# New call orders on four engines in a pre-norm attention and mixture-of-experts kernel, and a bias written four times by its transfer

## The reference

```
def _L0_attn_ref(x, Wq, Wk, Wv):
    q = jnp.einsum('bnd,de->bne', x, Wq)
    k = jnp.einsum('bnd,de->bne', x, Wk)
    v = jnp.einsum('bnd,de->bne', x, Wv)
    scores = jnp.einsum('bqe,bke->bqk', q, k)
    scores = jnp.where(causal, scores, -jnp.inf)
    attn = jax.nn.softmax(scores / jnp.sqrt(jnp.float32(k.shape[-1])), axis=-1)
    return jnp.einsum('bqk,bke->bqe', attn, v)

def _L0_ffn_ref(x, shared_gate, shared_up, shared_down, gate_w, up_w, down_w, router_w, routing_bias):
    shared = down(silu(gate(x)) * up(x))              # one expert for all tokens
    logits = jnp.einsum('bsh,eh->bse', x, router_w) + routing_bias
    scores, indices = jax.lax.top_k(jax.nn.sigmoid(logits), 2)
    scores = scores / jnp.sum(scores, axis=-1, keepdims=True)
    ...                                               # the two chosen of 8 experts, weighted
    return shared + combined

x = x + _L0_attn_ref(_layernorm(x), Wq, Wk, Wv)
x = x + _L0_ffn_ref(_layernorm(x), ...)
```

## Time and profile before

| | us |
|---|---|
| median of three runs | 547.94 |
| lowest and highest of them | 544.14, 548.08 |
| the profiled execution | 547.93 |
| its span | 546.2 |
| TensorE busy in the span | 512.3 (94%) |
| VectorE, ScalarE, GpSimd busy | 323.0, 308.4, 283.1 |

### The profile page before, as it was taken

How to read it: one execution, slowest core, us unless ns; L and a number is a source line. 1 busy time by engine, 2 the same in 40 slices (tenths; PEclk the granted TensorE clock), 3 DMA queues, 4 the chain that set the end, 5 groups by cost and what they waited for, 6 DMA issues and landing times.

```text
span 546.2 us, 15135 instructions
## 1 busy us (share of the span) xinstructions
PE 512.3 (94%) x4869; PEld 423.5 (78%) x4869; DVE 323.0 (59%) x918; ACT 308.4 (56%) x588; POOL 283.1 (52%) x237
## 2 busy tenths in 40 slices
PE   4798998899999999999999999999999999999992
PEld 3465776688887888888767789888798888888881
DVE  4788999688988788898645334334243332343331
ACT  3889896678877757675243444444444433444341
POOL 3347776768787765865033244353533525345444
PEclk9899999899999999999999999999999999999997
DMA  8399875989694967446558675665854756446443
GB/s 266 77 223 181 171 180 107 197 251 198 179 199 141 199 171 123 133 149 188 134 91 106 83 110 74 90 82 77 105 69 72 82 64 89 57 66 79 61 61 38
DMA packets 139351, 68.55 MB, mean 126 GB/s; under 512 B 114608, under 2 KB 132336, under 8 KB 139280
## 3 DMA queue, kind: packets, MB, share of 16 engines
q1 hardware_dynamic: 126128, 48.84, 45.7%
q0 software_dynamic: 13152, 18.76, 19.6%
HBM read 19.46 MB, written 23.08 MB: 78 GB/s over the span
## 4 chain that ended last, share of the span: by engine, by line
PE 68%; DMA 8%; DVE 7%; ACT 5%; SPq 5%; issue 4%; POOL 2%; POOLq 0%; ACTq 0%; DVEq 0%
PE bank L2252 31%; PE bank L2276 16%; PE bank L2585 4%; PE bank L2358 3%; PE bank L2383 2%; PE bank L2602 2%; PE bank L2405 2%; PE bank L2663 2%; DMA x<-rows 2%; PE bank L2428 2%; SPq L420 2%; DMA v<-xnrow 2%; DMA wst<-w_all 1%; DMA ptr<-phl 1%; DMA xn2t<-xrow 1%
## 5 line engine op out<-in xcount | busy, mean ns | idle before, releaser
L2252 PE MATMUL bank<-xn2t,w 128*128 128x256 f16 x1608 | 185.5, 273 | 1.6 <-DVE th L1676 1.3
L2252 PEld LDWEIGHTS bank<-xn2t,w 128*128 (+1 forms) x1608 | 155.3, 98 | 22.7 <-DVE th L1676 1.9
L1676 DVE SCALAR_TENSOR_TENSOR th<-th,bank 128x512 f32<-128x512 f32 x83 | 56.8, 685 | 68.7 <-ACT th L1002 64.5
L2276 PE MATMUL bank<-w,h 128*128 (+1 forms) x768 | 92.2, 272 | 0.3
L1002 ACT ACTIVATE th<-bank 128x512 f32<-128x512 f32 x83 | 49.4, 596 | 61.9 <-PE bank L2252 54.6
L2276 PEld LDWEIGHTS bank<-w,h 128*128 128x128 f16 x768 | 73.1, 98 | 9.6 <-issue 0.3
L875 POOL DMA_INDIRECT out<-p,wm x28 | 44.4, 1587 | 65.1 <-ACT p L1333 24.0
L1489 DVE TENSOR_TENSOR h<-th,h 128x512 f16<-128x512 f32 (+1 forms) x69 | 47.1, 683 | 45.2 <-ACT h L952 44.9
L952 ACT ACTIVATE h<-th 128x512 f16<-128x512 f32 (+1 forms) x69 | 42.9, 622 | 53.2 <-DVE th L1676 31.5
L771 POOL DMA_INDIRECT rows<-xrow,sidx x56 | 59.0, 1054 | 16.5 <-issue 13.3
L749 POOL TENSOR_TENSOR w<-wst,w 128x768 f16<-128x768 f32 x32 | 52.7, 1647 | 19.7 <-ACT w L952 19.5
(11 more groups left out here) (193 smaller groups left out, 792.4 us busy)
## 6 DMA issues: line engine op xcount, KB each, us to landing
wst<-w_all SPq DMA_DIRECT2D x36, 384.0 KB, 4.1
x<-x SPq DMA_DIRECT2D x8, 512.0 KB, 5.8
out<-x SPq DMA_DIRECT2D x8, 512.0 KB, 3.8
rows<-x POOLq DMA_DIRECT2D x1, 1192.5 KB, 8.6
rows<-xrow,sidx POOLq DMA_INDIRECT x56
out<-p,wm POOLq DMA_INDIRECT x28
xn2t<-rows SPq DMA_TRANSPOSE x26, 3.9
wm<-rows SPq DMA_DIRECT2D x26, 9.0 KB, 2.6
```

Source lines behind the costliest of these rows:

```text
L1676: d.scalar_tensor_tensor(out=tb, in0=tb, scalar=1.0 / WS if by_silu(t) else 0.5 / (WS * WS), in1=U[half][:, :], op0=ALU.mult, op1=ALU.mult ...
L2252: ins = mm(dst, w_ap(j, ws, m * MAT + k * I + (2 * half + i) * P, P), moving(ms * KD + k), start=(cnt == 0), stop=(cnt == 3 * KD - 1))
L2276: ins = mm(o[:, a * D:(a + 1) * D], hb[:, (hs * KI + i) * TT + a * P:(hs * KI + i) * TT + (a + 1) * P], w_ap(j, ws, 2 * MAT + i * D, D), s ...
```

## The change

TensorE's list is not touched. The bias transfer writes all four copies, has a semaphore of its own (`bias_in`), and is issued after four loads of x; `bias_rows` is gone, and `router_high` waits for the router alone. Everything else is order. In the lists of VectorE, ScalarE, GpSimd and SyncE calls are moved in the opening and in `iteration(i)`; no call but `bias_rows` is added or removed, save one more wait on GpSimd (`shift2`) in the opening. The lists of the last batch and of the routed experts stay.

```
-            sp.dma_start(biases[:, 0:E], bias.partition_broadcast(P)).then_inc(small_in, 16)
             x_load(1)
             w_load(0)
             x_load(2)
+            w_load(1)
             x_load(3)
-            w_load(1)
+            sp.dma_start(biases[:, :].rearrange("p (n e) -> p n e", n=NB),
+                         bias.partition_broadcast(P).unsqueeze(1).to_broadcast([P, NB, E])).then_inc(bias_in, 16)
+            x_load(4)
             xn_transpose(1)
...
             p_transpose(0, 2)
+            xn_transpose(2)
             p_transpose(0, 3)
-            xn_transpose(2)
             w_load(4)
-            x_load(4)
             w_load(5)
...
             p_transpose(1, 2)
+            p_transpose(1, 3)
             w_load(6)
-            p_transpose(1, 3)
-            x_load(5)
-            w_load(7)
             xn2_transpose(0, 0)
             xn2_transpose(0, 1)
+            w_load(7)
+            xn_transpose(3)
             w_load(8)
-            xn_transpose(3)
             p_transpose(2, 0)
+            x_load(5)
             w_load(9)
-            xn2_transpose(1, 0)
             p_transpose(2, 1)
             w_load(10)
+            xn2_transpose(1, 0)
             xn2_transpose(1, 1)
             p_transpose(2, 2)
+            w_load(11)
             p_transpose(2, 3)
-            w_load(11)
             w_load(12)
 
             def iteration(i):
 
+                w_load(4 * i + 1)
                 out_base(i - 3)
-                w_load(4 * i + 1)
                 xn2_transpose(i - 1, 0)
+                xn2_transpose(i - 1, 1)
                 w_load(4 * i + 2)
-                xn2_transpose(i - 1, 1)
                 p_transpose(i, 0)
+                p_transpose(i, 1)
                 xn_transpose(i + 1)
-                p_transpose(i, 1)
                 p_transpose(i, 2)
                 p_transpose(i, 3)
                 w_load(4 * i + 3)
+                x_load(i + 3)
                 w_load(4 * i + 4)
-                x_load(i + 3)
...
@@ GpSimd
             w_low(2)
             w_low(3)
+            rstd1(3)
             rstd2(0)
+            pool.wait_ge(shift2, 1)
             w_low(4)
-            w_low(5)
             xn2_low(0, 0)
             xn2_low(0, 1)
+            w_low(5)
+            rstd1(4)
+            xn_low(3)
             w_low(6)
-            xn_low(3)
             rstd2(1)
-            rstd1(4)
             w_low(7)
...
@@ ScalarE
             exp_of(0, 2)
+            xn_high(2)
             p_high(0, 2)
+            w_scale(2)
+            t_high(1, 0)
             exp_of(0, 3)
-            xn_high(2)
+            t_high(1, 1)
             p_high(0, 3)
-            t_high(1, 0)
-            w_scale(2)
-            t_high(1, 1)
+            w_scale(3)
             w_high(2)
-            w_scale(3)
+            exp_of(1, 0)
             w_high(3)
-            exp_of(1, 0)
+            exp_of(1, 1)
             p_high(1, 0)
-            exp_of(1, 1)
             p_high(1, 1)
             exp_of(1, 2)
+            v_high(1, 0)
+            w_scale(4)
             p_high(1, 2)
-            v_high(1, 0)
             v_high(1, 1)
-            w_scale(4)
             w_high(4)
             t_high(2, 0)
-            w_scale(5)
             exp_of(1, 3)
             p_high(1, 3)
-            w_high(5)
...
-            def bias_rows():
-
-                dve.wait_ge(small_in, 32)
-                for i in range(1, NB):
-                    ins = d.tensor_copy(biases[:, i * E:(i + 1) * E], biases[:, 0:E])
-                ins.then_inc(bias_rdy, 1)
...
@@ VectorE
             first_xn_normalise()
+            stats_1(1)
             wm_low()
-            stats_1(1)
             aggregate_1(1)
...
             t_low(1, 1)
+            p_low(0, 3)
+            row_max(1, 0)
             add_attention(0, 0, 1)
-            row_max(1, 0)
-            bias_rows()
             minus_max(1, 0)
...
             v_low(1, 0)
             shift_2(0)
+            row_sums(1)
             p_low(1, 3)
+            t_low(2, 0)
             v_low(1, 1)
             stats_1(4)
-            t_low(2, 0)
-            row_sums(1)
...
             ffn_gate(1, 1)
             read_logits(1)
+            add_attention(2, 0, 1)
+            p_low(2, 3)
             ffn_up(1, 1)
             add_attention(2, 1, 2)
             route(1)
+            weights(1)
             ffn_low(1, 0)
-            weights(1)
             add_attention(2, 2, 3)
+            add_attention(2, 3, 4)
             add_shared(0)
-            add_attention(2, 3, 4)
-            ffn_low(1, 1)
             stats_2(2)
             aggregate_2(2)
-            places(1)
-            t_low(3, 1)
+            ffn_low(1, 1)
             v_low(3, 0)
             shift_2(2)
+            t_low(3, 1)
+            places(1)
```

More of the change, by code:

```diff
@@ L1168, in _ @@
             xn2_high(0, 1)
-            w_scale(6)
-            w_high(6)
+            w_scale(5)
+            w_high(5)
             xn_normalise(3)
             xn_high(3)
+            w_scale(6)
+            exp_of(2, 0)
+            p_high(2, 0)
             v_high(2, 0)
-            exp_of(2, 0)
+            w_high(6)
+            exp_of(2, 1)
             v_high(2, 1)
-            p_high(2, 0)
-            exp_of(2, 1)
             w_scale(7)
@@ L1206, in _ @@
             xn_normalise(4)
-            xn_high(4)
             w_scale(11)
             w_high(11)
+            w_scale(12)
             v_high(3, 0)
+            xn_high(4)
+            w_high(12)
+            v_high(3, 1)
             t_high(3, 1)
-            v_high(3, 1)
-            w_scale(12)
-            w_high(12)
             xn2_normalise(2, 0)
@@ L1221, in iteration @@
                 exp_of(i, 0)
+                xn2_high(i - 1, 1)
                 p_high(i, 0)
-                xn2_high(i - 1, 1)
                 tanh(2 * i - 4, 0)
+                w_scale(4 * i + 1)
                 exp_of(i, 1)
+                w_high(4 * i + 1)
                 p_high(i, 1)
                 exp_of(i, 2)
-                p_high(i, 2)
                 split_h(2 * i - 4, 0)
@@ L1905, in _ @@
             row_max(0, 1)
+            v_low(0, 0)
             minus_max(0, 1)
+            row_max(0, 2)
             p_low(0, 0)
-            row_max(0, 2)
+            v_low(0, 1)
+            p_low(0, 1)
             minus_max(0, 2)
-            p_low(0, 1)
             row_max(0, 3)
@@ L1913, in _ @@
             p_low(0, 2)
-            v_low(0, 1)
+            row_sums(0)
             aggregate_1(3)
-            row_sums(0)
-            p_low(0, 3)
             t_low(1, 0)
             t_low(1, 1)
+            p_low(0, 3)
+            row_max(1, 0)
             add_attention(0, 0, 1)
-            row_max(1, 0)
-            bias_rows()
             minus_max(1, 0)
```

217 lines of the change are left out of this document (106 added, 111 removed).

## The result

The kernel before has a median of 547.1 us over 19 runs (544.14 to 552.31), the changed one 550.15 over 19 (547.01 to 553.58). The ratio is 1.0063, with a 95% interval from 1.0043 to 1.0082: 3 us slower, where 4.4 faster was forecast. The profiled execution took 552.7 us; its span is 551.0, against 546.2. It is one of the longer ones, 2.6 us above its median, where the profiled one of before is 0.8 above its own: the two profiles differ by 4.8 us and the medians by 3.0, so a part of what the profile shows may be missing in other runs.

A forecast was written before the change was run, and what follows sets the result against it. TensorE bounds the kernel, busy 512.3 of 546.2 us. Terms: 0 at 45, +1.0 at 50, -2.0 at 71, +2.5 at 84, +2.2 and +1.2 at `logits(2)`: 4.9, less 0.5; 547.9 - 4.4 = 543.5 us, range 541 to 545.5.

The forecast's parts named there:

- Iterations 3 to 6 ... Zero.: Iterations 3 to 6: no TensorE idle to gain, about 2.4 us of slack before `pv(4,2)` for later `p_low(i,3)`; zero change.
- its own signs: Wrong if `pv(1,0)` moves over 1.5 us, `logits(2)` still waits 2 us, or TensorE idles in iterations 3 to 6.
- The slower rival: Iterations: work behind `read_logits(i-1)` outlasts the slack, `pv(i,2)` waits 2 us in each of four; 551.5 us, chance 0.13.
- Step 1: Start of the opening: `t_product(0)` some 0.3 us earlier (0 to 0.6); the larger bias transfer costs nothing.
- Step 2: Opening, bias copies removed: up to 1.8 us freed, 0 if GpSimd's hold passes on to `minus_max`.
- Steps 3 and 4: Opening: net 0 (-1.5 to +1.5) at `pv(1,0)` near 45.2; then +1.0 us (0 to 1.4) at `pv(1,3)`, transpose earlier.
- Step 5: Batch 1's `xn2`: transposes behind `w_load(10)` stall `logits(1)`, 1.0 us later than before, a step of -2.0 (0 to -4).
- Step 6: Batch 2's norm: `scores(3)` 1.5 us earlier; at `logits(2)` +2.2 from its wait and +1.2 from the clock drop.

The follow-up runs named there:

- stand-ins: Kernels, before and after included, whose DMA transposes are replaced by plain copies of the same bytes, same queue and semaphores: 540.69 us for before, 546.20 for after.
- h5: Small kernel without the layer, VectorE's subtraction started inside GpSimd's instruction by small operations ahead: six take 1.97 us beside GpSimd's subtraction, fourteen 1.12 beside one indirect DMA.
- s3: Changed kernel's opening with the old iteration order of all four engines, transposes as plain copies: 538.93 us, ratio 0.9848 to the kernel before.
- t2: Changed opening with the old iterations of all four engines again, transposes as plain copies, on another chip: 542.50 us, ratio 0.9803 to the kernel before.
- u2: Changed kernel with GpSimd's `rstd2(i)` moved ahead of `w_low(4i+3)`, transposes as plain copies: 547.01 us, ratio 0.9988 to the kernel before.
- s5: Changed kernel with VectorE's `ffn_low(2i-3,1)` moved back ahead of `weights(i-1)`, transposes as plain copies: 547.28 us, ratio 1.0008 to the kernel before.
- s8: Changed kernel with ScalarE's old iteration order alone, transposes as plain copies: 542.84 us, ratio 0.9899 to the kernel before.
- t3: Changed kernel with ScalarE's `w_scale(4i+1)` and `w_high(4i+1)` moved back to later places, transposes as plain copies: 552.45 us, ratio 1.0010 to the kernel before.
- s7: Changed kernel with VectorE's old iteration order alone, transposes as plain copies: 554.04 us, ratio 1.0114 to the kernel before.
- s4: Old kernel's opening with the new iteration order of all four engines, transposes as plain copies: 548.44 us, ratio 1.0011 to the kernel before.
- h4: Small kernel without the layer, VectorE's subtraction beside GpSimd's subtraction or indirect DMAs: VectorE's took 0.68 us in every case, GpSimd's 2.16 beside it and 1.64 otherwise.
- t4: Changed kernel once more with transposes as plain copies, otherwise unedited: 555.80 us, ratio 1.0060 to the kernel before.

## Why the prediction was wrong

**The step that failed is the last: "Iterations 3 to 6 ... Zero."** By its own signs the prediction was wrong if TensorE idled there, and it did. The step asked whether TensorE had idle to give and whether `pv(4,2)` had slack for a later `p_low(i,3)`. `pv(i,2)` indeed never waited. It didn't ask where VectorE's two-input subtractions would fall against GpSimd's in the new lists. The opening's held operations were priced; the iterations' were not, because before they cost TensorE nothing. Their cost was 0 by position only: `ffn_low(5,1)` led `w_low(19)` by 2.8 us. In its place the runs show 2.53 us of wait and 1.6 us of slow matmuls in one iteration of the real kernel's profile, and some 7 us over four iterations in the stand-ins. The slower rival had nearly the right size (551.5; 0.13) by luck: it had the work behind `read_logits` delaying `pv(i,2)` four times, and it was a hold delaying `shared_down(2i-3,1)`. Nor is the 2.4 us of slack for `pv(4,2)` worked out from the row that it names; the run shows only that `pv(i,2)` had enough.

**Step 1, size off, harmless.** `t_product(0)` came at 15.43, 0.68 later instead of 0.3 earlier, but `t_product(1,0)` was level again (26.89 against 26.96). Stand-ins with this same opening had it between 14.05 and 15.50: this start isn't set by the order alone. The bias landed 11.5 us after its issue (5.4 before), 41 us ahead of its reader: nothing, as said.

**Step 2, right.** `exp_of(1,0)` started at 34.59, and `minus_max(1,0)` ran inside GpSimd's two `w_low`:

```profile
34.42 0.14 DVE L1745 TENSOR_SCALAR nm<-mx 128x1 f32<-128x1 f32 x1
...
34.36 3.24 POOL L750 TENSOR_TENSOR w<-wst,w 128x768 f16<-128x768 f32 x2 [3.52 <-ACT w L954]
```

The Trainium skill ("SBUF — State Buffer", on ports and contention) has `tensor_scalar` contend only "when their operands meet the conditions" of the two-port mode, which the prediction left out. In h5 the same operation with four elements per partition is held (six take 1.97 us); with one element, in the row above, it isn't.

**Steps 3 and 4, right.** `pv(1,0)` at 46.00 (45.2 forecast, waiting for `v` as said), `pv(1,3)` without its idle, +1.09 for +1.0.

**Step 5, right loss, wrong cause.** `logits(1)` came at 72.86, 2.59 late, where 1.0 was said, but without an idle for `xn2t`. The loss was the wait of 2.46 for `mask` at 63.50, with the clock at half behind it from 63.36 to 66.77. The step followed `w_load(10)` and the transposes behind it, but not `w_load(7)`, which had moved behind the transposes of batch 0 and so came late to ScalarE, where `logits_exp(0)` stands behind `w_scale(7)` in both kernels, now with `xn2_normalise(1,0)` (1.0 us) ahead of it as well.

**Step 6, half.** `logits(2)` lost its wait and its clock drop: from `scores(3)`, 1.64 late, to 2.24 early at 102 is 3.9, for 2.2 + 1.2. But `scores(3)` was late, not 1.5 early: `pv(2,3)` waited 1.51 for its transpose (80.08), where nothing was said of it. At 102 us the sum stood at 2.24, for 4.4 forecast. (The step's own numbers, TensorE there at 95.9 and the transpose at 96.5, leave a wait of 0.6, so 1.9 and not the 2.2 that went into the sum.)

So about half of the forecast gain came in the opening, in the one profile of each; s3 and t2 show only that this opening costs nothing. The iterations took it and more. The stand-ins show this loss to be one of fit: ScalarE's new list readies `w_low(4i+1)` early, VectorE meets it, then meets `w_low(4i+3)`. That u2 and s5 free the held subtraction, and gain little as the next operation is held, is shown; that the early `w_low(4i+1)` is what begins it is argued from s8 and t3, and t3 is disturbed. Neither VectorE's nor GpSimd's list set back by itself helps; ScalarE's does, for what seems the larger part. How the 3 us of the real kernel divide among its lists stays open, as all of this was seen on stand-ins.

## What to carry to other kernels

Where a stretch shows no idle, its order may still be free only by position: before you move calls there, list the operations of VectorE and GpSimd that can hold each other, with the lead of each over the other, and ask which falls inside which afterwards. Lists of engines that feed each other are changed together or not at all; half of a good reordering (s7) was worse than either whole. A held operation wasn't mended by moving it: the next one took its place (s5, u2), and it would, until the holder stands where VectorE has nothing that TensorE needs.

## What the runs showed of the hardware

- A GpSimd subtraction of 1.64 us queued right behind an indirect DMA held VectorE 2.1 us (h5, after), and one behind `rstd` 2.07 (s4); the indirect DMA by itself held nothing (h5).
- VectorE's subtraction, started 0.02 us ahead of GpSimd's, made that one 2.17 instead of 1.64 (h4).
- Waits of 2.46 and 2.53 us of TensorE (after) were followed by 3.41 us at half clock, and so were those of 2.02 and 2.05 in t4, but not its wait of 2.00; in s4 and s5 not even those of 2.53 and 2.58 were, nor one of 3.47 in u2 at 76.60. The price of such a wait is itself uncertain by 1.6 us, what the slow stretch cost in iteration 4.
- In t3 the semaphore raised by the second half of `pv` went up 2.1 to 2.9 us after the record of its last matmul ended, in each of the four iterations, and VectorE waited for it; in the kernel before it went up within 0.02. All four traces of that chip have late signals of TensorE; no stand-in's trace of another chip has one.
